# Narrow cross-attention: one row tile of TensorE for each of a pair's two heads, maxima of two banks reduced by one operation

## What is computed

```python
q = split_heads(queries @ Wq)          # (4, 16, 256, 16)
k = split_heads(keys @ Wk)             # (4, 16, 4096, 16)
v = split_heads(values @ Wv)
scores = jnp.einsum('bhqd,bhkd->bhqk', q, k) / jnp.sqrt(jnp.float32(hd))
mask = jnp.arange(skv)[None, None, None, :] < valid_lens[:, None, None, None]
scores = jnp.where(mask, scores, NEG)
p_attn = jax.nn.softmax(scores, axis=-1)
out = jnp.einsum('bhqk,bhkd->bhqd', p_attn, v)
```

## Time and profile before

| | us |
|---|---|
| runs before, median of 3 (lowest, highest) | 4327.76 (4327.47, 4329.01) |
| the profiled execution | 4329.77 |
| its span in the profile | 4327.1 |
| prologue of the narrow attention | 2640 to 2733 |
| its 32 steps | 2733 to 3778 |

### The profile page before, as it was taken

One profiled execution on the slowest core, in us unless ns is written; L12 is line 12 of the kernel. 1 busy time (PEld: TensorE's weight loads), 2 busy tenths in 40 slices (PEclk: granted clock), 3 DMA queues, 4 the chain that ended last, 5 costly groups with the idle time before them and its releaser, 6 DMA issues. The chain is left out here.

```text
span 4327.1 us, 75594 instructions
## 1 busy us (share of the span) xinstructions
PE 3896.4 (90%) x27192; PEld 2768.8 (64%) x27192; DVE 2700.6 (62%) x4077; ACT 2460.7 (57%) x4518; POOL 1633.4 (38%) x1301
## 2 busy tenths in 40 slices
PE   5899999999999999999677985899999999967399
PEld 2677777777777777776445974555555555433288
DVE  5766666666666666664174213677777777658577
ACT  3577777777777777776142112455555556625165
POOL 1566666666666666666222002100000000014033
PEclk9999999999999999999797997999999999979699
DMA  5777777776777766663213566644444422100011
GB/s 200 269 253 250 245 255 253 250 255 240 265 252 250 247 238 224 228 226 118 65 20 120 197 230 209 191 147 138 143 147 140 137 69 66 34 23 1 12 50 42
DMA packets 232719, 724.99 MB, mean 168 GB/s; under 512 B 44556, under 2 KB 129804, under 8 KB 163724
## 3 DMA queue, kind: packets, MB, share of 16 engines
q1 hardware_dynamic: 229664, 711.78, 48.3%
q0 software_dynamic: 2688, 8.39, 0.5%
HBM read 625.70 MB, written 94.37 MB: 166 GB/s over the span
## 5 line engine op out<-in xcount | busy, mean ns | idle before, releaser
L752 POOL TENSOR_TENSOR wa_acc<-wa_acc,wa_probs 128x512 f32<-128x512 f32 x960 | 1246.4, 1298 | 526.8 <-ACT wa_probs L613 446.4
L677 DVE TENSOR_REDUCE wa_mx<-wa_ps_m 128x2 f32<-128x1024 f32 x512 | 626.8, 1224 | 486.5 <-PE wa_ps_m L488 486.3
L613 ACT ACTIVATE wa_probs<-wa_ps_s 128x512 f32<-128x512 f32 x1024 | 556.0, 595 | 528.9 <-PE wa_ps_s L534 523.6
L1204 ACT ACTIVATE na_probs<-na_ps_s 128x512 f32<-128x512 f32 x1024 | 564.2, 599 | 379.1 <-PE na_ps_s L1108 373.7
L1256 DVE TENSOR_REDUCE na_mx<-na_ps_m 128x1 f32<-128x512 f32 x1024 | 643.5, 682 | 187.7 <-PE na_ps_m L1093 186.7
L605 ACT ACTIVATE wa_ps_s<-wa_m_wide 128x512 f32<-128x512 f32 x1024 | 575.4, 605 | 1.0
L510 PE MATMUL wa_ps_o<-wa_probs,wa_values 128*64 128x256 f32 x4096 | 507.3, 390 | 0.0
L1093 PE MATMUL na_ps_m<-na_keys,na_q 98*128 98x512 f32 x1024 | 425.1, 423 | 43.6 <-DVE na_mx L1256 30.2
L1108 PE MATMUL na_ps_s<-na_q,na_keys 100*128 100x512 f32 x1024 | 430.4, 428 | 2.4 <-ACT na_probs L1204 1.5
L449 PE MATMUL wa_ps_k<-wa_k_ctx,wa_w_k 128*128 128x512 f32 x1488 | 388.3, 396 | 0.0
L475 PE MATMUL wa_ps_v<-wa_w_v,wa_v_ctx 128*128 128x256 f32 x2880 | 383.1, 282 | 0.0
(11 more groups left out here) (342 smaller groups left out, 5503.6 us busy)
## 6 DMA issues: line engine op xcount, KB each, us to landing
wa_k_ctx<-ctx_split SPq DMA_DIRECT2D x248, 1024.0 KB, 5.1
wa_v_ctx<-ctx_split SPq DMA_DIRECT2D x120, 1024.0 KB, 5.8
na_ctx<-ctx_split SPq DMA_DIRECT2D x56, 1024.0 KB, 6.9
na_keys<-k_rows SPq DMA_DIRECT2D x192, 256.0 KB
ctx_split<-wa_stage SPq DMA_DIRECT2D x32, 1024.0 KB, 9.1
wa_land<-in_ctxT SPq DMA_DIRECT2D x32, 512.0 KB, 9.9
ge_w_b<-in_w_rows SPq DMA_DIRECT2D x8, 2048.0 KB
k_rows<-na_k_high SPq DMA_DIRECT2D x64, 256.0 KB, 2.3
```

The costliest lines, as they stand in the source:

```text
L613: act.activation(probs[:, c % R:c % R + 2, h * SQ:(h + 1) * SQ], ps_s[n % BANKS][:, :].rearrange("p (c n) -> p c n", c=2), ACT.Exp).then_i ...
L677: dve.tensor_reduce(mx[:, half, :, k], ps_m[:, :, :], AX.X, ALU.max).then_inc(m_taken, 1)
L752: pool.tensor_tensor(acc[:, :], acc[:, :], probs[:, c % R, :], ALU.add).then_inc(summed, 1)
L1204: act.activation(probs[:, n % RP, :], ps_s[n % RS][:, :], ACT.Exp).then_inc(exp_done, 1)
```

## The change

Every head gets 64 rows of the array. Its 52 rows (4 of mask and shift, 48 of high and low parts) begin at row 0 for the first head and at row 64 for the second, so `q` needs no zeros and 256 columns for a head instead of 512. A step now has ST = 16 even or odd turns `t` of two chunks each. `scores(a, t)` is four matmuls of 256 columns, alternating between the heads: head 0 into bank `ps_s0`, head 1 into `ps_s1`, two chunks side by side in a bank. There are two such banks, not three, and `scores(a, t)` waits until the exponents of both banks of turn t - 1 are done (`exp_done`, 1 + n). `maximum` makes both heads' scores of a unit into two neighbouring banks, and one VectorE operation reduces 128 x 1024; there are 16 units and two such pairs of banks. The weighing follows on odd turns, the last weighing of a pair moves behind turn 1 of the next pair, and projections move to even turns: keys to turns 6, 8, 10, 12 in halves, values to turn 14 and to turn 0 of the next step. The keys of a pair are loaded by 16 DMAs instead of 8.

```diff
-    MASK = 3 * W
-    MROWS, ROWS = MASK + 2, MASK + 4
+    HEAD = 64
+    KEYS = 4
+    ROWS = KEYS + 3 * DH
+    ST = CH // 2
...
-    RP, RS, RM = 12, 3, 3
+    RP = 12
...
-        q = [s.sb(f"q{i}", [P, 2, SQ], F32R) for i in range(3)]
+        q = [s.sb(f"q{i}", [P, SQ], F32R) for i in range(3)]
...
-        ps_s = [s.ps(f"ps_s{i}", [P, 512]) for i in range(RS)]
-        ps_m = [s.ps(f"ps_m{i}", [P, 512]) for i in range(RM)]
+        ps_s = [s.ps(f"ps_s{i}", [P, 512]) for i in range(2)]
+        ps_m = [s.ps(f"ps_m{i}", [P, 2, 512]) for i in range(2)]
...
-        def steps(c):
-            return (2 * c, 2 * c + 1) if c < 3 else (c + 3,) if c + 3 < CH else ()
+        def units(t):
+
+            return (0,) if t == 0 else (2 * t - 1, 2 * t) if t < 3 else (t + 2,) if t + 2 < ST else ()
...
-            def maximum(a, i):
-                u, j = divmod(i, 4)
-                n = a * CH + i
-                if i == 0:
+            def maximum(a, u):
...
+                pe.wait_ge(m_taken, 1 + max(n - 1, 0))
+                for h in range(2):
+                    r = slice(h * HEAD, h * HEAD + ROWS)
+                    ins = pe.matmul(ps_m[n % 2][:, h, :], q[a % 3][r, half * P:(half + 1) * P], keys[a % 2][r, k * 512:(k + 1) * 512],
+                                    start=True, stop=True)
+                ins.then_inc(m_done, 1)
...
-                for j in range(4):
-                    ins = pe.matmul(ps_m[((a + 1) * CH + 2) % RM][MASK:ROWS, j * P:(j + 1) * P], msplit[:, j, :].bitcast(F32),
-                                    ident[:, :], start=True, stop=True)
+                for half in range(2):
+                    for h in range(2):
+                        ins = pe.matmul(ps_m[1][h * HEAD:h * HEAD + 2, 0, half * P:(half + 1) * P],
+                                        msplit[:, 2 * half + h, :].bitcast(F32), ident[:, :], start=True, stop=True)
...
-            def scores(a, c):
-                n = a * CH + c
-                if c == 0:
-                    pe.wait_ge(q_ready, 1 + a + 1)
-                pe.wait_ge(exp_done, 1 + max(n + 1 - RS, 0))
-                pe.matmul(ps_s[n % RS][:, :], keys[a % 2][0:ROWS, c * P:(c + 1) * P],
-                          q[a % 3][0:ROWS, :, :].rearrange("p h n -> p (h n)"), start=True, stop=True).then_inc(s_ready, 1)
+            def scores(a, t):
+                n = a * CH + 2 * t
+                if t == 0:
+                    pe.wait_ge(q_ready, 1 + 2 * (a + 1))
+                pe.wait_ge(exp_done, 1 + n)
+                for i in range(2):
+                    for h in range(2):
+                        r = slice(h * HEAD, h * HEAD + ROWS)
+                        ins = pe.matmul(ps_s[h][:, i * SQ:(i + 1) * SQ], keys[a % 2][r, (2 * t + i) * P:(2 * t + i + 1) * P],
+                                        q[a % 3][r, :], start=True, stop=True)
+                        if i:
+                            ins.then_inc(s_ready, 1)
...
-                    pe.wait_ge(ov_ready, 1 + max(a - 1, 0))
+                    pe.wait_ge(ov_ready, 1 + a)
...
-                for c in range(CH):
-                    scores(a, c)
+                old = v_block(a - 1) if a else None
+                for t in range(ST):
+                    scores(a, t)
                     if a + 1 < G:
-                        for i in steps(c):
-                            maximum(a + 1, i)
-                    if c == 3 and a:
+                        for u in units(t):
+                            maximum(a + 1, u)
+                    if t == 1 and a:
+                        weigh(a - 1, CG - 1)
+                    elif t % 2 and t > 1:
+                        weigh(a, t // 2 - 1)
+                    if t == 0 and old is not None:
+                        pe.wait_ge(v_ready, 1 + 2 * old + 1)
+                        project_values(old, 1, ps_p)
+                    if t == 4 and a:
                         pe.wait_ge(masked, 1 + 2 * min(a + FIRST, N))
                         pe.wait_ge(v_ready, 1 + 2 * min(a + CG, N))
                         add_up(a - 1)
-                    if c == 12 and kb is not None:
+                    if t in (6, 8) and kb is not None:
                         pe.wait_ge(o_ready, 1 + a)
-                        project_keys(kb, 0, ps_p)
-                    if c == 18 and kb is not None:
+                        project_keys(kb, 0, ps_p, (t // 2 - 3,))
+                    if t in (10, 12) and kb is not None:
                         pe.wait_ge(masked, 1 + 2 * kb + 1)
-                        project_keys(kb, 1, ps_p)
-                    if c == 24 and vb is not None:
+                        project_keys(kb, 1, ps_p, (t // 2 - 5,))
+                    if t == 14 and vb is not None:
                         pe.wait_ge(o_ready, 1 + a)
                         pe.wait_ge(masked, 1 + 2 * min(a + FIRST + 1, N))
                         project_values(vb, 0, ps_p)
-                    if c % 4 == 1 and c > 4:
-                        weigh(a, c // 4 - 1)
-                if vb is not None:
-                    pe.wait_ge(v_ready, 1 + 2 * vb + 1)
-                    project_values(vb, 1, ps_p)
                 if a + 1 < G:
                     turn_maximum(a + 1)
-                weigh(a, CG - 1)
+            weigh(G - 1, CG - 1)
...
-            def exponents(a, c):
-                n = a * CH + c
-                act.wait_ge(s_ready, 1 + n + 1)
-                if n >= RP:
-                    act.wait_ge(pv_done, 1 + (n - RP) // 4 + 1)
-                act.activation(probs[:, n % RP, :], ps_s[n % RS][:, :], ACT.Exp).then_inc(exp_done, 1)
+            def exponents(a, t, h):
+                c = a * CH + 2 * t
+                act.wait_ge(s_ready, 1 + c + h + 1)
+                if c >= RP:
+                    act.wait_ge(pv_done, 1 + (c - RP) // 4 + 1)
+                act.activation(probs[:, c % RP:c % RP + 2, h * SQ:(h + 1) * SQ],
+                               ps_s[h][:, :].rearrange("p (c n) -> p c n", c=2), ACT.Exp).then_inc(exp_done, 1)
 
             def take_maximum(a):
                 act.wait_ge(mT_done, 1 + a + 1)
-                act.activation(q[a % 3][MASK:ROWS, :, :].rearrange("p h n -> p (h n)"), ps_m[((a + 1) * CH + 2) % RM][MASK:ROWS, :],
-                               ACT.Copy).then_inc(q_ready, 1)
+                for h in range(2):
+                    act.activation(q[a % 3][h * HEAD:h * HEAD + 2, :], ps_m[1][h * HEAD:h * HEAD + 2, 0, 0:SQ],
+                                   ACT.Copy).then_inc(q_ready, 1)
...
+                for t in range(ST):
+                    for h in range(2):
+                        exponents(a, t, h)
+                    if t == 1 and a and v_block(a - 1) is not None:
+                        take_values(v_block(a - 1), 1, ps_p)
+                    if t == 10 and kb is not None:
                         take_high(kb, 0)
-                    if c == 22 and kb is not None:
+                    if t == 14 and kb is not None:
                         take_high(kb, 1)
-                    if c == 28 and vb is not None:
+                    if t == 15 and vb is not None:
...
-                dve.tensor_reduce(mx[:, j, u:u + 1], ps_m[n % RM][:, :], AX.X, ALU.max).then_inc(m_taken, 1)
+                dve.tensor_reduce(mx[:, half, :, k], ps_m[n % 2][:, :, :], AX.X, ALU.max).then_inc(m_taken, 1)
...
-                if a:
-                    copy_out(a - 1)
-                for c in range(CH):
+                for t in range(ST):
+                    if t == 2 and a:
+                        copy_out(a - 1)
                     if a + 1 < G:
-                        for i in steps(c):
-                            take_maximum(a + 1, i)
-                    if c == 6 and a:
+                        for u in units(t):
+                            take_maximum(a + 1, u)
+                    if t == 4 and a:
                         divide(a - 1)
-                    if c == 14 and kb is not None:
+                    if t == 9 and kb is not None:
                         mask_keys(kb, 0, ps_p)
-                    if c == 20 and kb is not None:
+                    if t == 13 and kb is not None:
```

More of the change, by code:

```diff
@@ L946, in narrow_attention, with first_bank @@
             loads[True, n] = loads[False, n]
+        def first_bank(n, half):
+            return ps_m[1][:, 0, :] if half == 0 and n < 4 else ps_p
         @block.sync
@@ L1139, in _ @@
                 for half in range(2 if n < CG else 0):
[L1140 to L1141 removed]
+                    pe.wait_ge(v_ready, 1 + (2 * n + half if n >= 4 else max(2 * n + half - 1, 0)))
+                    project_values(n, half, first_bank(n, half))
                 if n >= 5:
[L1143 to L1146 removed]
+                    maximum(0, 2 * (n - 5))
+                    maximum(0, 2 * (n - 5) + 1)
+            for u in range(2 * (FIRST - 5), ST):
+                maximum(0, u)
             turn_maximum(0)
@@ L1215, in _ @@
                 for half in range(2 if n < CG else 0):
```

(12 more changed lines are left out.)

105 lines of the change are left out of this document (52 added, 53 removed).

## The result

The changed kernel takes 4320.24 us (median of 20 runs, 4307.58 to 4331.38) against 4327.88 us before (20 runs, 4321.08 to 4331.88): ratio 0.9982, interval 0.9976 to 0.9989. The forecast was 4261, with a range of 4232 to 4322. It is a gain, but one of 8 us where the forecast's sum had 69, and by the forecast's own bound of 0.2% it counts as no change.

A forecast was written before the change was run, and what follows sets the result against it. TensorE bound the kernel before; afterwards a PE-ACT ring would. Steps 1 to 20 -66.4, 21 to 30 -4.0, step 31 +4.9, step 0 -2.5, prologue -1: together -69 from 4329.8, likeliest 4261 us, range 4232 to 4322.

The forecast's parts named there:

- the ring of 1.68 us: Each turn: scores and exponents alternate between PE and ACT without a double buffer, 1.67 to 1.68 us a turn.
- the added waits in turns 1, 3, 10, 13/14 and 15: Longer turns in a step: +0.2, +0.8, +0.3, +1.0 (+0.4 without masks) and +1.2 us.
- a middle step of 30.95: Steps 1 to 20: 29.1 + 0.5 + 0.3 + 1.0 + 0.05 us each, against 34.27 before.
- stay the bound: Rival, all steps: TensorE stays the bound and all 7.5 us a step come in, 4090 us; 3 in 100.
- no turn of the ring grew by 0.1: Rival, all 512 turns: each 0.1 us longer from drains or semaphores, 51 us, 4312; upper part of the own case.
- I cost it at nothing: Key loads and moved stores on SP: no cost; if late by 2 us in each of 20 steps, 4301 us.
- the text's own signs of being wrong: Profile after: turns shorter than the ring's parts, clock at 0.50, or PE waiting for DMA at a step's start.
- the clock: Rival: idle TensorE drops to 1.2 GHz, 14 us more a step; eight late steps make 4376 us; 11 in 100.
- step 0: First step: like a middle step without the work carried over, waiting for the same keys; about 2.5 us shorter.
- turns 0.1 us longer and slower transposes: Upper end of the range: 0.1 us more a turn and transposes 0.35 us slower x 31, 4323 us.
- a transfer or handoff that I have not seen: Rival, middle steps: it eats the gain of 3.3 us in each, within 0.2% of 4328 us; 5 in 100.
- TensorE's floor: Late step bounded by TensorE: 20 or so us, 29 - 7.5 = 21.5, against 26.9 for the ring's 16 turns.

The follow-up runs named there:

- e2: The changed kernel with the first half of the keys of the pair after next loaded ahead of the store of the first projected half: 4283.12 us.
- f7: e2 with matmuls nobody reads, of the maxima's form, added in step 31: 4275.17 us.
- g2: e2 with DVE's masks ahead of the reductions, f7's added matmuls, and two more unread matmuls in turn 3 and after the shift of steps 24 to 30: 4246.88 us.
- g4: e2 with the first half of pair 1's keys issued ahead of the two context loads: 4278.47 us.
- g1: f6 with the weighing of two chunks in every turn in place of four in odd turns: 4295.36 us.
- h1: g2 with g4's key load, and g1's own waits and split weighing in steps 24 to 31 alone: 4228.19 us.
- f6: f5 with each head's scores waiting for that head's own exponent of the turn before, in place of both: 4274.80 us.
- f5: e2 with a turn's scores written head by head, both chunks of head 0, then both of head 1: 4285.31 us.
- b1: The kernel before with each of its three key loads of 32 rows in two of 16 rows: 4331.85 us.

## Why the prediction was wrong

**Right:** a pair of row tiles costs what one matmul cost; the ring of 1.68 us; the added waits in turns 1, 3, 10, 13/14 and 15, to 0.1 us; and with them a middle step of 30.95, measured 31.01 once the keys are early (30.85 in a step at full clock; two of the twenty had a stretch at half clock). Late steps undisturbed by the clock take 28.98 us, forecast 29.1. TensorE did not stay the bound, and no turn of the ring grew by 0.1.

**The step that failed: "I cost it at nothing", the loads of the keys.** I had counted eight issues where there were four and a later store, and had the lead right, about 8 us (8.4 measured). I let it cover the loads without a price for the issue, 3.4 us, or for a 16-row transfer, and did not ask what the lead had been: 14.1 us. Turn 0 takes 4.01 us where it takes 2.28 with early keys, and turn 1, with the clock behind it, 0.5 more. PE's own list puts 1.0 us a step down to the keys; part of the rest is half clock, and how much was not taken apart. e2 removes all of it for 37 us. The text gave 4301 for loads late by 2 us in each step, which is this term. What spoke for it was in view: stores and loads on one queue, and half the rows in each load. PE waiting for DMA at a step's start and a clock of 0.50 were the text's own signs of being wrong, and both came.

**Mis-sized: the clock.** I had made it a rival, with a step or more at 1.2 GHz, at 11 in 100, or nothing. It came in between: 8.0 us in step 31 (f7), and 302.8 - 293.9 = 8.9 us in steps 21 to 30 of e2, in stretches of a few us; with g2's matmuls they take 294.5. At half clock an even turn takes 1.97 us, the rival had 1.95; an odd one 2.56 in step 31, which has no maxima.

**Mis-sized: step 0,** forecast 2.5 us shorter, 36.6, and measured 40.5. I wrote that it waits for the same keys, and gave the wait no change. These keys are issued behind two context loads, and the wait got longer. The first maxima, before and after:

```profile
2739.76 1.19 PE L1093 MATMUL na_ps_m<-na_keys,na_q 98*128 98x512 f32 x2 [5.05 <-DMA na_keys<-edges]
```
```profile
2745.36 0.80 PE L1105 MATMUL na_ps_m<-na_keys,na_q 52*128 52x512 f32 x2 [8.63 <-DMA na_keys<-k_rows]
```

Loading them earlier takes 4.6 us off the time (g4), of which 3.1 are in step 0.

4261 + 37 + 8.0 + 8.9 + 4.6 = 4319.5, against 4320.2 measured. That it closes to 0.7 us is partly chance: the terms are differences of medians over runs that lie up to 24 us apart, and the stages ahead of step 0 and behind step 31 are not in it.

**What is luck.** 4320.24 lies inside the range of 4232 to 4322. Its upper end was made of turns 0.1 us longer and slower transposes, 4323 together; neither came, late keys and the clock filled their place. The rival "a transfer or handoff that I have not seen", given 5 in 100, has the time (within 0.2% of 4328) but only part of the mechanism: it was to eat all of the 3.3 us of a middle step, and the keys ate 1.9; and these loads were seen, and priced at nothing.

**TensorE's floor.** I had 20 to 21.5 us for a late step that TensorE bounds. With the ring open it takes 26.7 (g1) to 27.2 (h1). One part shows in g1: with own waits the heads' matmuls no longer start together, and the scores and maxima of a turn take 0.82 to 0.96 us in place of 0.67. The rest stays open; the changes between row tiles and column tiles may be in it, and were not measured alone.

## What to carry to other kernels

When a change shortens a stage, every load that was in time for the old length must be costed again, from its issue to its use (here 14.1 us became 8.4): count what stands ahead of it on its queue, and give small transfers a price of their own. When an engine stops being the bound, ask what its clock does with the idle time; filling a wait with matmuls nobody reads was worth 33 us here. And an edit that opens a wait can pay in one stage and cost in another: own waits with split weighing took the late steps from 29.2 (g2) to 27.3 us (h1), while splitting the weighing took the middle ones from 30.9 (f6) to 33.2 (g1). Give it only to the stages where it pays.

## What I had not expected of the hardware

- Matmuls of two row tiles ran in twos in both orders tried: in f5, written head by head, the maxima start 0.34 us behind the first score, as when written in pairs. In f6 and g1, where each head waits for its own exponent, they did not in every turn: the four scores from 3571.13 on in g1 start at 3571.127, .349, .427 and .651. The Trainium skill, TensorEngine Tiling (Array Packing), section Key Properties, says that tiles operate independently; the trace agrees.
- Splitting 32-row loads in two, same bytes, raised the queue's share from 46.9 to 60.6% (b1).
- In e2's late steps, with TensorE busy for 160 of 214 us and waiting in the shift and in turn 3, the clock fell to 1.2 GHz for short stretches; with two matmuls in each of these waits its mean there rose from 0.95 to 0.99 (g2). In step 31 it was 0.57 in e2 and 1.00 with more matmuls (f7).
